# AdaLN and ternary FFN on one core: W2 in two loads on ScalarE's queue, x's first half scaled in two parts, the products by input blocks

## The reference, cut to what matters

```python
# x (128, 32, 256), cond (128, 128), W3 (128, 256), W2 (256, 256), w1 and w3 (682, 256), w2 (256, 682), float32
q_emb = relu(cond @ W3 + b3)
y = (n * x + x.sum(axis=1, keepdims=True)) * q_emb[:, None, :]     # n = 32
c = relu(y @ W2 + b2)
w1q, w3q, w2q = ternary(w1), ternary(w3), ternary(w2)   # clip(round(w / mean|w|), -1, 1) * mean|w|
out = x + (silu(c @ w1q.T) * (c @ w3q.T)) @ w2q.T
```

## Time and profile before

| | |
|---|---|
| median of 3 runs | 165.48 us (165.42 to 166.0) |
| the profiled execution | 166.24 us |
| its span, from the first to the last instruction | 164.5 us |
| TensorE busy | 159.8 us, 97% of the span |
| VectorE busy | 116.7 us, 71% |
| ScalarE busy | 89.7 us, 55% |
| GpSimd busy | 55.1 us, 34% |
| read and written in HBM | 8.32 MB and 4.19 MB |

### The profile page before, as it was taken

The page is one execution under the profiler, slowest core; times in us unless marked ns, Lnnn a source line. Parts: engine busy times, 40 slices in busy tenths (PEclk is TensorE's granted clock), DMA queues, the critical chain, the costliest instruction groups (busy, mean ns, idle before and its releaser), DMA issues.

```text
span 164.5 us, 2300 instructions
## 1 busy us (share of the span) xinstructions
PE 159.8 (97%) x767; PEld 131.7 (80%) x767; DVE 116.7 (71%) x185; ACT 89.7 (55%) x165; POOL 55.1 (34%) x53
## 2 busy tenths in 40 slices
PE   7899999999999999999999999999999999999992
PEld 4788687888887888788887888788887888788892
DVE  2258999988978891888548891888648870566863
ACT  3159788525744466355844466355744566255540
POOL 5014033312361276204841266204841267001600
PEclk9999999999999999999999999999999999999999
DMA  5999656666566698000150006000160006000063
GB/s 149 276 349 190 98 92 98 99 100 101 83 97 96 90 222 152 8 0 0 29 99 0 0 4 117 13 0 0 25 105 4 2 0 111 17 0 4 16 112 128
DMA packets 67412, 12.67 MB, mean 77 GB/s; under 512 B 63216, under 2 KB 67144, under 8 KB 67400
## 3 DMA queue, kind: packets, MB, share of 16 engines
q1 hardware_dynamic: 67104, 12.33, 38.2%
q10 hardware_dynamic: 296, 0.20, 0.5%
HBM read 8.32 MB, written 4.19 MB: 76 GB/s over the span
## 4 chain that ended last, share of the span: by engine, by line
PE 95%; DMA 2%; ACTq 1%; DVE 0%; issue 0%
PE bank L543 49%; PE bank L586 21%; PE bank L473 17%; PE bank L570 3%; DMA b_rows<-in_L_cond_b_dram 2%; PE bank L449 2%; PE bank L488 1%; PE bank L500 0%; ACTq L315 0%; PE bank L482 0%; ACTq L314 0%; PE bank L447 0%; DVE xo L793 0%; ACTq L313 0%; PE bank L513 0%; PE bank L461 0%
## 5 line engine op out<-in xcount | busy, mean ns | idle before, releaser
L543 PE MATMUL bank<-c_hi,T 128*128 128x512 f32 (+1 forms) x176 | 69.2, 393 | 0.0
L543 PE MATMUL bank<-c_lo,T 128*128 128x512 f32 (+1 forms) x176 | 68.8, 391 | 0.0
L393 ACT ACTIVATE silu<-bank,checked 128x512 f32<-128x512 f32 (+1 forms) x48 | 33.0, 688 | 51.6 <-PE bank L543 51.5
L778 DVE SCALAR_TENSOR_TENSOR gf<-bank,out_scale,silu 128x512 f32<-128x512 f32 (+1 forms) x42 | 31.3, 745 | 34.5 <-PE bank L543 30.8
L543 PEld LDWEIGHTS bank<-c_hi,T 128*128 128x128 f32 (+1 forms) x176 | 32.8, 186 | 7.6 <-issue 0.2
L543 PEld LDWEIGHTS bank<-c_lo,T 128*128 128x128 f32 (+1 forms) x176 | 32.8, 186 | 7.3
L271 POOL TENSOR_TENSOR x<-y,qT 128x512 f32<-128x512 f32 x12 | 13.7, 1143 | 53.3 <-DVE y L690 53.3
L473 PE MATMUL bank<-x,W_sb 128*128 128x256 f32 x128 | 29.5, 381 | 0.0
L586 PE MATMUL bank<-g_hi,T 128*128 128x512 f32 x70 | 28.5, 407 | 0.0
L786 DVE TENSOR_TENSOR g_lo<-gf,g_hi 128x512 fp32r<-128x512 f32 x40 | 28.5, 712 | 0.0
L400 ACT CAST g_hi<-gf 128x512 fp32r<-128x512 f32 x40 | 24.5, 612 | 5.4 <-DVE gf L778 5.1
(11 more groups left out here) (78 smaller groups left out, 111.4 us busy)
## 6 DMA issues: line engine op xcount, KB each, us to landing
xb<-in_x_dram SPq DMA_DIRECT2D x64, 64.0 KB, 2.5
out_dram<-turned SPq DMA_DIRECT2D x28, 128.0 KB, 2.7
xo<-in_x_dram SPq DMA_DIRECT2D x3, 256.0 KB, 5.1
w_sb<-in_L_ffn_w_dram SPq DMA_DIRECT2D x2, 384.0 KB, 6.0
w_sb<-in_L_ffn_w_dram SPq DMA_DIRECT2D x1, 682.0 KB, 7.8
w_sb<-in_L_ffn_w_dram SPq DMA_DIRECT2D x2, 256.0 KB
xo<-in_x_dram SPq DMA_DIRECT2D x1, 512.0 KB, 4.4
xo<-in_x_dram SPq DMA_DIRECT2D x2, 128.0 KB, 2.5
```

What stands on the lines that cost most here:

```text
L393: nc.scalar.activation(silu[r, m % 2, :], h1[j % 2][r], ACT.Silu, scale=checked[r, 0:1]).then_inc(silu_done, 1)
L543: last = pe.matmul(dst[j % 2][0:w, :], T13[:, k, col:col + w], part[:, g % NC, k, :], start=(i == 0), stop=(i == len(passes) - 1))
L778: nc.vector.scalar_tensor_tensor(out=gf[r, m % 3, :], in0=second, scalar=out_scale[r], in1=silu[r, m % 2, :], op0=ALU.mult, op1=ALU.mult). ...
```

## The change

W2 becomes two loads of one input block each, 128 KB, with a semaphore each, on ScalarE's queue behind the biases. The biases move up to second place there. W3 moves to SyncE's queue, between the two tiles of half 0. qT is made by VectorE in two instructions, behind its copy of `b_cols`, in place of two activations on ScalarE. The scaling of half 0 becomes two instructions, one for each input block, each with its own count of `x1_done`; all later counts of that semaphore are one higher. `project_c` runs over input blocks k outside and output blocks c inside, for all halves; for half 0 it waits for W2's block k and for the scaled block k ahead of each k. One filler fewer stands ahead of `mix_x(1)`, and the two behind it are gone.

```diff
-            for t in range(HTT):
-                sp.dma_start(kept(0)[:, t], x_v[0, :, t]).then_inc(got_first[t], 16)
+            sp.dma_start(kept(0)[:, 0], x_v[0, :, 0]).then_inc(got_first[0], 16)
+            sp.dma_start(W3_sb[:], W3).then_inc(got_W3, 16)
+            sp.dma_start(kept(0)[:, 1], x_v[0, :, 1]).then_inc(got_first[1], 16)
             load_half(1)
-            sp.dma_start(W2_sb[:], W2.rearrange("(c p) n -> p c n", p=P)).then_inc(got_W2, 16)
             load_half(2)
...
             act.dma_start(cond_sb[:], cond).then_inc(got_cond, 16)
-            act.dma_start(W3_sb[:], W3).then_inc(got_W3, 16)
             act.dma_start(b_rows[0:DC, :], b3.rearrange("(c p) -> c p", p=P)).then_inc(got_b, 16)
             act.dma_start(b_rows[DC:2 * DC, :], b2.rearrange("(c p) -> c p", p=P)).then_inc(got_b, 16)
+            for k in range(DC):
+                act.dma_start(W2_sb[:, k], W2[k * P:(k + 1) * P, :]).then_inc(got_W2[k], 16)
...
             act.wait_ge(b_cols_copied, 1)
-            act.wait_ge(q_done, DC)
-            for c in range(DC):
-                nc.scalar.activation(qT[:, :, c, :], qT_ps[:, c, :].rearrange("p (h b) -> p h b", b=HB), ACT.Relu,
-                                     bias=b3_col[c]).then_inc(q_ready, 1)
...
             def project_c(n):
-                pe.wait_ge(x1_done, n + 1)
+                if n:
+                    pe.wait_ge(x1_done, n + DC)
...
-                for c in range(DC):
-                    for k in range(DC):
+                for k in range(DC):
+                    if n == 0:
+                        pe.wait_ge(got_W2[k], 16)
+                        pe.wait_ge(x1_done, k + 1)
+                    for c in range(DC):
                         last = pe.matmul(z[:, c, :], W2_sb[:, k, c * P:(c + 1) * P], x1[:, n % 2, k, :],
-                                         start=(k == 0), stop=(k == DC - 1))
+                                         start=(k == 0 and c == 0), stop=(k == DC - 1), skip_group_check=True)
...
             mix_x(0)
-            keep_busy(4)
+            keep_busy(3)
             mix_x(1)
-            keep_busy(2)
-            pe.wait_ge(got_W2, 16)
             project_c(0)
...
+                if n == 0:
+                    for k in range(DC):
+                        nc.vector.tensor_tensor(by_batch(x1[:, 0, k]), by_batch(mixed_of(0)[:, k * HT:(k + 1) * HT]),
+                                                qT[:, 0, k].unsqueeze(2).broadcast_to([P, HB, S]), ALU.mult).then_inc(x1_done, 1)
+                    return
...
             nc.vector.tensor_copy(b_cols[:], b_cols_ps).then_inc(b_cols_copied, 1)
+            dve.wait_ge(b_cols_copied, 1)
+            dve.wait_ge(q_done, DC)
+            for c in range(DC):
+                nc.vector.tensor_scalar(qT[:, :, c, :], qT_ps[:, c, :].rearrange("p (h b) -> p h b", b=HB), b3_col[c], 0.0,
+                                        ALU.add, ALU.max).then_inc(q_ready, 1)
             dve.wait_ge(q_ready, DC)
```

More of the change, by code:

```diff
@@ L147, in z_of @@
             return bank[:, b, :].rearrange("p (c n) -> p c n", c=DC)
-        got_cond, got_W3, got_W2, got_b = sem("got_cond"), sem("got_W3"), sem("got_W2"), sem("got_b")
+        got_cond, got_W3, got_b = sem("got_cond"), sem("got_W3"), sem("got_b")
+        got_W2 = [sem(f"got_W2_{k}") for k in range(DC)]
         got_w1, got_w3 = [[sem(f"got_w{k}_{part}") for part in range(2)] for k in (1, 3)]
@@ L283, in _ @@
             pool.wait_ge(early_lo_done, 1)
-            pool.wait_ge(x1_done, EARLY)
+            pool.wait_ge(x1_done, EARLY - 1 + DC)
             for n in range(1, EARLY):
@@ L430, in mix_x @@
                 if n == 3:
-                    pe.wait_ge(x1_done, 2)
+                    pe.wait_ge(x1_done, 1 + DC)
                 if n == 2:
@@ L528, in _ @@
             project_c(2)
-            pe.wait_ge(x1_done, EARLY - 1)
+            pe.wait_ge(x1_done, EARLY - 2 + DC)
             transpose_w13(0, 0, w1_t)
@@ L596, in output_step @@
                     output_share(m, b, {2 * b + t: o[b][:, t, :] for t in range(2)})
-            pe.wait_ge(x1_done, EARLY)
+            pe.wait_ge(x1_done, EARLY - 1 + DC)
             pe.wait_ge(T1_copied, 1)
@@ L687, in add_sum @@
                 if n >= EARLY:
-                    dve.wait_ge(x1_done, max(n - 1, SUMMED + 1))
+                    dve.wait_ge(x1_done, max(n - 2, SUMMED) + DC)
                 nc.vector.scalar_tensor_tensor(
```

## The result

The changed kernel takes 166.51 us in the median of 22 executions (165.98 to 168.37). The kernel before, run beside it in the same series, takes 165.98 us in the median of 22 (165.41 to 166.85). The medians differ by 0.53 us. The ratio, which is not that of the two medians, is 1.0045, 95% interval 1.0026 to 1.0064: slower by 0.45%, clear of noise though under the 0.5% bound of the forecast. The forecast was 165.4 us in a range up to 166.0, and 166.51 lies above that range. The 165.48 us on which it was built was a median of 3. All ratios leave out single executions of over 1.5% above the fastest of the same kernel: none of the changed kernel's 22, but one of e4_idle, one of g1_w3_act, both high ones of f4_loads_before_fill and the three high ones of before.

A forecast was written before the change was run, and what follows sets the result against it. The bias rows were taken as the bound, with half 1 of x 0.4 us behind. `project_c(0)` 0.06 us earlier, called about 0.1, took the median from 165.48 to 165.4 us, range 164.7 to 166.0.

The forecast's parts named there:

- Rival C: TensorE idles from about 4.5 to 4.87, matmul clock stays at 1.2 GHz until `project_c(0)`: 166.5 us, chance 0.05.
- I take its sum as a shift of the profiled execution and apply the same shift to the median: The sum over the first 8 us was taken off both the profiled 166.24 us and the median 165.48 us.
- The 0.06 us of gain at `project_c(0)`: After `mix_x(1)`, `project_c(0)` was to issue at 7.88 against 7.94, with half 1 landing at 6.85.
- the 0.76 us between the profiled execution and that median: The profiled execution of the kernel before took 166.24 us, the median of its runs 165.48 us.
- When half 1 lands: Half 1 of x, ahead of `mix_x(1)`: said to land between 6.8 and 7.15, taken as 6.85, against 6.48.
- B: Rival: W2 on the second queue takes bandwidth, half 1 lands at 7.3 to 7.9: 165.9 to 166.5 us, chance 0.15.
- the 6.91 of break-even: Landing time of half 1, ahead of `mix_x(1)`, at which the change would neither gain nor lose.
- Tile 1 of half 0: Second tile of x's first half: issued third at about 1.75, to land 2.8 us later at 4.55.
- the late copy: ScalarE's copy of condT, which `project_q` waits for, was to end at 4.63 in place of 4.15.
- the order by input blocks at no cost: `project_c`: the same eight instructions and 1.78 us for each half, so the new order was costed at nothing.
- the stretch from `project_c(0)` to the end: All work after `project_c(0)` issues was to take the same 156.6 us as before.
- Later needs: Nearest later load, w3's first part, lands at 11.97, needed at 13.01: 1.04 us margin, so the shift reaches the end.

The follow-up runs named there:

- e4_idle: The changed kernel without the two fillers ahead of `mix_x(0)` and the three ahead of `mix_x(1)`; ratio 1.0043, 5 of 12 executions from 167.44 to 168.42 us.
- g1_w3_act: The kernel of f3 with w3's three loads on ScalarE's queue behind the copy of condT; 168.39 us median, ratio 1.015.
- f4_loads_before_fill: The kernel of e3_compute with four fillers behind `project_q`; 166.25 us median, two executions at 168.22 and 168.34, ratio without these two 0.9999.
- e2_loads: The kernel before with only the new loads of the changed one; 167.89 us median, ratio 1.0101, four of six executions from 167.84 to 168.12.
- e1: The changed kernel with three fillers ahead of `project_q` and twelve in place of three ahead of `mix_x(1)`; 166.17 us median, ratio 1.0021.
- f1: The changed kernel with three fillers ahead of `project_q` alone; 166.01 us median of 11, ratio 1.0011.
- f2: The changed kernel with twelve fillers in place of three ahead of `mix_x(1)` alone; 166.48 us median, ratio 1.0054, 3 of 12 from 168.26 to 168.43.
- h1: The changed kernel with W2 in one load on ScalarE's queue in place of two; 166.31 us median, ratio 1.0027.
- g2: The kernel of f3 with W2 in one load in place of two; 165.68 us median of 12, ratio 0.999.
- f3: The changed kernel with W2's two loads on SyncE's queue behind half 1 in place of ScalarE's; 166.06 us median, ratio 1.001.
- e3_compute: The changed kernel with the loads of the kernel before, all other parts of the change kept; 165.58 us median, ratio 0.9983.

## Why the prediction was wrong

**Rival C had too low a chance and too low a price.** I gave it 0.05 and 166.5 us. The upper group has 6 of 22 executions, 1.8 us above the lower group (168.07 against 166.25); that all six are C is not shown, since the one high profile is of e2_loads. My price was 1.06 us, with the lower level up to 9.0. In e2_loads it holds to 9.7, into `project_c(0)`, which starts 1.57 us later than before (9.67 against 8.10). That the median is 166.51, the very number given for C, is luck: the executions that C would explain lie near 168, and the median lies inside the lower group. The idle stretch that goes with the group is the one I named (TensorE idle while the copy of condT is late). My argument against C, that an idle stretch of 0.73 us at 5.2 leaves the clock up today, was about the wrong moment: in the profile before that stretch lies after the clock has come up at 4.7, while this one can lie ahead of it. e1, f1 and f2 together point to it. By the Trainium skill, page "TensorE: Matmul & The Clock Gate", part 1, the moment of the rise also varies from run to run, by about 0.5 us either way. The profiles of this case agree that it varies and show more: 3.7 to 6.8 us in thirteen of them, with `project_q` at 1.2 GHz in the second profile of before and partly above it in the first. I read that rule only for the level, not for its spread.

**One profiled execution was taken for the median.** The step "I take its sum as a shift of the profiled execution and apply the same shift to the median" failed. The execution of before that was profiled took 166.24 us, above the later median of 165.98, and in it the biases and half 1 were late (5.91, 6.48). The second profile of the same kernel had half 1 at 4.9 and no wait for either, and the two kernels with the same loads had it at 6.2 and 6.1: 6.48 was the latest of four. The 0.06 us of gain at `project_c(0)` was computed from the latest case of before against a usual case of after (6.26 to 7.05 in seven profiles with W2 on ScalarE's queue, 6.6 in the mean). In the lower group the changed kernel is 166.25 - 165.98 = 0.27 us behind in place of 0.1 ahead; that half 1 beside W2 makes this is argued from h1 and g2, not shown by itself.

The miss of 1.1 us at the median (166.51 for 165.4) adds up so: 0.5 from the base (165.48, a median of 3, for 165.98), 0.1 of gain that did not come, 0.27 in the lower group, and 0.26 from there to the median of all 22, which is the upper group's doing. The base made up nearly half of it, and the 0.76 us between the profiled execution and that median, which I noted and passed over, was a sign of how far executions of one kernel lie apart.

**When half 1 lands** was right for the changed kernel (6.85 said, 6.70 in the profile), and the reason given under B fits. With the same issue time and W2 behind half 1 on SyncE's queue it lands at 5.05 and 5.75. B was called decisive from 7.74 on; in truth it works at 6.7, because before is often better than the 6.91 of break-even. Tile 1 of half 0 was placed too early: 4.55 said, and 1.78 + 3.6 = 5.38 in the profile after, just ahead of its matmuls at 5.43; in h1 it landed at 5.98 and was waited for. By the Trainium skill, page "DMA: Bandwidth & Descriptors", section "Queues, rings and completion order", the two issuing queues take turns on the same engines. Three runs agree with it: half 1 took 2.8 us in f3 and 4.8 in h1, and half 3 took 8.2 in g1.

**Right as told:** the late copy (4.53 against 4.63 said), the bias transpose at 5.28 without a wait, W3 no bound, qT and the two half scalings on VectorE (0.61 and 0.76 us for 0.58 and 0.86) done before `mix_x(1)` is, the order by input blocks at no cost (1.73 us for eight), the stretch from `project_c(0)` to the end (156.5 us for 156.6). e3_compute shows the parts other than the loads together 0.3 us faster than before. Which of them gives that wasn't tried.

**Later needs** held for the change, and not for f3: with two more issues ahead of the FFN weights w3 becomes the bound.

**Open.** What decides whether an execution falls into the upper group is not settled: f4 has two such executions and before three of 118 without the idle stretch. That filling the stretch takes the group away rests on 0 of 23 against 18 of 52, where the 52 are of four kernels and e2_loads alone gives 4 of 6; the clock as its cause was seen in one profile, that of e2_loads. No upper execution of the changed kernel itself was profiled.

## What to carry to other kernels

Profile more than one execution, or at least ask where the profiled one lies among the times, before a wait of a few tenths in it is taken for the kernel's bound; and look at the list of times, not only at its median. Count every transfer issued on an engine's queue as time of what that engine does next: two loads moved onto ScalarE's list, with one taken off, made a copy 0.38 us late and opened an idle stretch on TensorE, at a time when its clock isn't up yet in some executions. A load on a second queue isn't ahead of the first queue's, it is beside it; the one that is needed first should have the bandwidth alone.

## What the runs showed of the hardware

An idle stretch of 0.2 to 0.4 us on TensorE ahead of 4.67 goes with 18 of 52 executions that are about 2 us longer, and in the one of these that was profiled the 1.2 GHz level held until 9.7 us although TensorE was busy in the chain without a gap from 0.99 on. In the thirteen other profiles the level rose between 3.7 and 6.8 us. The column of the granted clock reads 1.00 through all of it: the trace of e2_loads has its first record of the clock at 9.72, that of the changed kernel at 3.76, and the column counts the time ahead of it as full. So the level has to be read from the spacing of the matmuls. A load of 256 KB issued at 2.25 us landed after 2.8 and 3.5 us with only cond and the biases on the other queue (f3, g2), and after 4.0 to 4.8 us with W2 there. With W3 and the biases there (the loads of before, issued at 1.78) it took between 3.1 and 4.7 us, a spread that no run here explains.
